# A graph network on one core: count and weight matrices by blocks of 8 destination nodes

## The reference

```python
# L0, three times: mean over the edges of each relation
seg = dst * R + etype
agg = segment_sum(x[src], seg) / max(count, 1)
h = relu(einsum('nrd,rdk->nk', agg, W) + h @ root + bias)
# L1: attention over edges, weight exp(-leaky_relu(s1[src] + s2[dst]))
h_prime = segment_sum(edge_e[:, None] * h[dst], src)
# L2: weighted sum over edges
agg = segment_sum(edge_weight[:, None] * x[row], col);  y = agg @ W.T + b
# L3: mean of edge attributes per node, then an MLP on [x, mean]
agg = segment_sum(edge_attr, col) / max(cnt, 1)
```

## Time and profile before

| | |
|---|---|
| median of 3 runs | 5356.65 us (5346.82 to 5359.11) |
| span of the profiled execution | 5385.6 us |
| PE busy | 4150.9 us, 77% |
| DVE busy | 2954.1 us, 55% |
| GpSimd busy | 3014.2 us, 56% |
| ScalarE busy | 964.9 us, 18% |
| front | 0 to 649 us |
| pass 1 | 649 to 1745 us |
| pass 2 | 1775 to 2757 us |
| pass 3 | 2773 to 3740 us |
| attention | 3740 to 4055 us |
| pass 4 | 4083 to 5215 us |

### The profile page before, as it was taken

How to read it: one execution, slowest core, us unless ns; L and a number is a source line. 1 busy time by engine, 2 the same in 40 slices (tenths; PEclk the granted TensorE clock), 3 DMA queues, 4 the chain that set the end, 5 groups by cost and what they waited for, 6 DMA issues and landing times.

```text
span 5385.6 us, 98227 instructions
## 1 busy us (share of the span) xinstructions
PE 4150.9 (77%) x20763; PEld 2938.9 (55%) x20764; DVE 2954.1 (55%) x6694; ACT 964.9 (18%) x3611; POOL 3014.2 (56%) x3064
## 2 busy tenths in 40 slices
PE   4777677778888788888878788887766988898863
PEld 1223265666666555555545555555665766676652
DVE  5444333333322677777777777877893333333335
ACT  0111111111111111111211111112441111111112
POOL 0000066666665677777767777775005777777750
PEclk7678778777777999999999999999785555656666
DMA  2011233333344222222322222322442333333320
GB/s 73 27 44 49 74 97 115 120 115 120 117 123 124 74 71 71 85 92 94 105 89 71 71 82 88 95 94 85 148 157 83 104 103 102 101 103 103 101 71 12
DMA packets 318265, 492.02 MB, mean 91 GB/s; under 512 B 98090, under 2 KB 221228, under 8 KB 314556
## 3 DMA queue, kind: packets, MB, share of 16 engines
q0 software_dynamic: 108864, 246.74, 16.0%
q1 hardware_dynamic: 209372, 244.94, 13.7%
HBM read 406.11 MB, written 85.29 MB: 91 GB/s over the span
## 4 chain that ended last, share of the span: by engine, by line
PE 30%; DMA 26%; issue 19%; POOL 12%; DVE 8%; DVEq 2%; ACT 2%; POOLq 1%; ACTq 0%; SPq 0%
DMA msg_r<-y_tab,idx_r 21%; POOL msg_r L494 12%; PE psum L1452 6%; DMA msg_r<-z_tab,idx_r 4%; PE psum L1387 4%; PE psum L1597 3%; PE psum L1598 2%; PE psum L1267 1%; PE psum L1279 1%; DVE hot_r L983 1%; DVE h_t L1142 1%; PE psum L1549 1%; PE psum L1399 1%; PE psum L1414 1%; PE psum L1299 1%
## 5 line engine op out<-in xcount | busy, mean ns | idle before, releaser
L494 POOL DMA_INDIRECT msg_r<-y_tab,idx_r x2160 | 2163.1, 1001 | 1561.7 <-issue 1185.3
L1452 PE MATMUL psum<-shot_r,hotb_r 128*128 128x400 bf16 x5760 | 1221.9, 335 | 359.2 <-DMA msg_r<-y_tab,idx_r 318.9
L494 POOL DMA_INDIRECT msg_r<-z_tab,idx_r x882 | 844.4, 957 | 630.8 <-issue 584.8
L1452 PEld LDWEIGHTS psum<-shot_r,hotb_r 128*128 128x128 bf16 x5760 | 480.3, 98 | 760.4 <-DMA msg_r<-y_tab,idx_r 404.0
L1007 DVE TENSOR_SCALAR shot_r<-iota_h,edge_g 128x1600 bf16<-128x1600 f16 x1440 | 893.6, 675 | 0.0
L570 ACT COPY idx_r<-row_i 128x1 int32 x2142 | 410.0, 191 | 2456.9 <-DMA msg_r<-y_tab,idx_r 2337.2
L1597 PE MATMUL psum<-msg_r,shot_r 128*128 128x128 f32 x1764 | 636.3, 460 | 143.7 <-DMA msg_r<-z_tab,idx_r 107.3
L1387 PE MATMUL psum<-hot_r,msg_r 128*128 128x128 f32 x2880 | 575.0, 358 | 194.3 <-DMA msg_r<-y_tab,idx_r 101.1
L1387 PEld LDWEIGHTS psum<-hot_r,msg_r 128*128 128x128 f32 x2880 | 486.5, 253 | 300.6 <-DMA msg_r<-y_tab,idx_r 158.3
L1597 PEld LDWEIGHTS psum<-msg_r,shot_r 128*128 128x128 f32 x1764 | 414.3, 292 | 339.2 <-DMA msg_r<-z_tab,idx_r 284.9
L1598 PE MATMUL psum<-msg_r,hot_r 128*128 128x128 f32 x1764 | 521.9, 396 | 0.0
(11 more groups left out here) (276 smaller groups left out, 3795.1 us busy)
## 6 DMA issues: line engine op xcount, KB each, us to landing
msg_r<-in_attr SPq DMA_DIRECT2D x882, 64.0 KB
h_t<-count_tab SPq DMA_DIRECT2D x25, 1600.0 KB, 6.5
count_tab<-w_s SPq DMA_DIRECT2D x48, 800.0 KB, 3.7
msg_r<-y_tab,idx_r POOLq DMA_INDIRECT x2160, 2.7
xn<-heavy_tab SPq DMA_DIRECT2D x76, 320.0 KB
y_tab<-y_s SPq DMA_DIRECT2D x25, 640.0 KB, 2.9
xn<-y_tab SPq DMA_DIRECT2D x25, 640.0 KB, 4.1
y_tab<-y_s SPq DMA_DIRECT2D x50, 320.0 KB
```

What stands on the lines that cost most here:

```text
L494: pool.indirect_dma_start(out=msg_r[:, q, 0:width], out_offset=None, in_=table, in_offset=bass.IndirectOffsetOnAxis(ap=idx_r[:, q:q + 1], ...
L1452: ins = T.matmul(psum[:, 4 + b, 0:CB], hotb_r[:, q, :], shot_r[:, q, b * CB:(b + 1) * CB], start=first, stop=last)
```

## The change

Count and weight matrices are built in another way, by *windows*: a window is 8 destination nodes (D8 = 8), and there are 384 (NW) for tiles 1 to 24. The edges of a window lie in a few neighbouring chunks, which are taken two at a time (VR = 2): one such step is a *visit*. For a visit DVE makes, for two chunks, `low` (the source's place within its tile, 128 columns), `key` (destination within the window times source tile, KW = 200 columns) and `weighted` (key times edge weight, 200), all f32, in one buffer `see_r`. PE multiplies `low` by the 400 columns of the other two and adds over the visits. So the first 200 columns are counts, the other 200 sums of weights. ScalarE copies both out of PSUM; the weights go to a new table `w_tab`; the counts are transposed on PE (`window_turn`), copied again and go to `count_tab`.

```diff
+            def window_hots(x):
+
+                w = x[2]
+                v0, v1, c0 = window_visits(dve, x)
+                behind = dve.snap(c0 - v0 * 2)
+                with dve.Fori(v0, v1) as v:
...
+                    dve.wait_ge(s_seen, v)
+                    V.scalar_tensor_tensor(out=key, in0=pair(KEY, KW), scalar=win_base[:, bass.ds(w, 1)],
+                                           in1=iota[:, None, 0:KW].broadcast_to([P, VR, KW]), op0=ALU.subtract, op1=ALU.is_equal)\
+                        .then_inc(s_key_hot, 1)
+                    V.tensor_tensor(out=low, in0=iota[:, None, 0:P].broadcast_to([P, VR, P]), in1=pair(LOW, P), op=ALU.is_equal)
+                    alone(dve)
+                    dve.wait_ge(s_key_hot, v)
+                    V.tensor_tensor(out=weighted, in0=key, in1=pair(WGT, KW), op=ALU.mult).then_inc(s_see, 1)
...
+            def window_sums(x):
+
+                v0, v1, _ = window_visits(pe, x)
+                alone(pe)
+                pe.wait_ge(s_turned, x[0] + 1)
+                clear(win_ps)
+                with pe.Fori(v0, v1) as v:
+                    alone(pe)
+                    pe.wait_ge(s_see, v)
+                    for i in range(VR):
+                        last = T.matmul(win_ps, see_r[:, i, 0:P], see_r[:, i, P:P + 2 * KW], start=False, stop=False)
+                    last.then_inc(s_seen, 1)
+                close(win_ps, s_wsum)
```

```diff
@@ PE, group_sums
+                    if q == UH - 1:
+                        if k < 3:
+                            window_sums(x)
+                if k < 3:
+                    window_turn(x)
@@ ScalarE, one_group
+                for q in range(U):
+                    if k == 2 and q % UH == 0:
+                        plain_ones(b, q // UH)
+                    if chunk is not None:
+                        next_row(k, of, c0, before16, q)
+                    if q == UH:
+                        window_out_of_psum(x)
+                    if q == UH + 1:
+                        window_store(x)
+                turned_out(x)
@@ PE, removed from passes 2 and 3
-                for b in range(4):
-                    ins = T.matmul(psum[:, 4 + b, 0:CB], hotb_r[:, q, :], shot_r[:, q, b * CB:(b + 1) * CB],
-                                   start=first, stop=last)
@@ DVE, removed from passes 2 and 3
-                    for q in range(half.start, half.stop):
-                        V.tensor_scalar(out=shot_r[:, q, :], in0=iota_h[:, :], scalar1=edge_g[:, SRC, q:q + 1], scalar2=None,
-                                        op0=ALU.is_equal)
```

```diff
@@ PE, pass 3
             def chunk2(q, slot, first, last):
-                count_sources(2, q, first, last)
+                T.matmul(attr_acc(slot), one_r[:, q, :], msg_r[:, q, P:2 * P], start=False, stop=False)
                 return T.matmul(acc(slot), hot_r[:, q, :], msg_r[:, q, 0:P], start=False, stop=False)
```

Pass 4 gathers only for tile 0 (27 groups), from x itself. Its groups are dealt out over 24 shares. In each share one tile D of 1 to 24 is computed as a product of x with the tile's 16 windows, loaded in one piece of 1.6 MB (128 × 16 runs of 800 bytes) into one of two slots; the weight matrix of L2 comes behind it:

```diff
+            def wide(t, slot):
+
+                pe.wait_ge(s_win_in[slot], t * 16 + 16)
+                for i in range(TILES):
+                    last = T.matmul(psum[:, 2 + slot, 0:P].rearrange("p (w d) -> p w d", w=WPT), xn[:, i, :], w_in[slot][:, :, i * D8:(i + 1) * D8],
+                                    start=i == 0, stop=i == TILES - 1)
+                last.then_inc(s_dense, 1)
+
+            def new_x(n, D, slot):
+
+                to = psum[:, 4 + slot, 0:P]
...
+                T.matmul(to, stage[:, slot, 0, :], l2w_s[:, :], start=True, stop=False)
+                T.matmul(to, ones[0:1, :], row("l2_b")[0:1, :], start=False, stop=False)
+                T.matmul(to, ident[:, :], xn[:, bass.ds(D, 1), :].rearrange("p o f -> p (o f)"), start=False, stop=True).then_inc(s_l2, 1)
```

More of the change, by code:

```diff
@@ L508, in _ @@
             pool.wait_ge(s_z_out, 16)
[L509 removed]
+            gather(3, x_tab, P, groups, 0)
         @block.scalar
@@ L598, in gathering @@
+                with act.Fori(begin + 1, TILES - 1) as D:
+                    tile(D)
+                tile(TILES - 1, ahead=False)
                 if table is not None:
```

662 lines of the change are left out of this document (434 added, 228 removed).

## The result

The changed kernel takes 7416.29 us, median of 4 runs (7396.35 to 7436.28), against 5357.88: a ratio of 1.384 (95% interval 1.380 to 1.388). The direction was forecast, the size was not: 2058 us more, not 723, and above the end of the range (6550).

The account below looks back on a forecast made before the run. Each pass was taken as a ring: a group costs the larger of the gathers' 7.5 us and the DVE-PE chain. 5385.6 + 955 + 343 + 258 - 860 + 25 = 6107, less 29: about 6080 us; range 5450 to 6550.

Parts of the forecast that it names:

- pass 4: Only 27 groups of tile 0 instead of 147: near 300 us, a change of -860 (bounds -925, -710).
- the attention stage: Between passes 3 and 4, the same count_tab loads hidden under the tile before: change 0, at most some 3 us later start.
- in pass 1 the mechanism: Pass 1: VectorE and TensorE work in series, 11.85 us per one-visit group, 3.95 per further visit; +955 (bounds +650, +1350).
- Rival (a): Passes 1 to 3: windows hidden under the gathers' 7.5 us per group, so faster, 4670 us; chance 0.15.
- Rival (c): Pass 4: window loads from 800-byte runs bound it, 14 to 18 us per tile, +40 to +130, 6150 us; chance 0.07.
- the sum keeps the row's 2.6: VectorE's prologue ahead of a window, four table reads and addresses: 2.6 us from a three-load row (bounds 1.6, 3.5).
- TensorE's reads counted at nothing: TensorE's own table reads ahead of a window in passes 1 to 3: no time in the sum.
- at the 0.77 of pass 1 about 2.05 with its start: TensorE's part of a visit, four matmul instructions: 1.5 us at high clock, 2.9 at low, taken as 2.05.
- Rival (b): All passes: TensorE falls to its low clock, visits 2.9 instead of 2.05 us, total 6900 us; chance 0.08.
- the chain of pass 3: Pass 3: ScalarE's plain_ones and work ahead add 1.8 to 2.1 us, 9.8 per group; +258 (bounds +35, +410).
- pass 2's chain: Pass 2: chunks 3 to 5, VectorE's half, prologue, hots, visit, close: 7.85 us per group; +343 (bounds +140, +470).
- the front: Ahead of the first matrix stage: 28 operations, 13.5 us, and a prefix sum with copies, 11.7; +25 (bounds +15, +30).

Follow-up runs that it names:

- the shorter reads: Changed kernel, reads left in place: fourth number read once ahead of the passes, TensorE skips chunk number, VectorE reads it without bounds; 7053.85 us against 7587.51.

## Why the prediction was right or wrong

**Right: the direction, pass 4 and the attention stage, and in pass 1 the mechanism.** There windows stand in a serial chain VectorE, TensorE, VectorE behind one buffer: the chain shows it, moving VectorE's reads gave back nearly the whole prologue, and with the buffer handed over in two halves a further visit got shorter. Rival (a), which put the group under 7.5 us, needed the opposite; with the reads and the place of the window mended, pass 2 still took 12.6 us per group. Pass 4 took 311 us for a predicted 300. Rival (c) did not occur: a window load took 8.0 us from issue to landing, a tile 13 us, and TensorE waited for such a load once, for 11.5 us. The loop behind pass 3, forecast to run 0 times, did run once (385 copies out, 581 visits for 579), some 16 us.

**Wrong: the prologue, "the sum keeps the row's 2.6".** It measured 3.98 us in pass 1, outside the upper bound of 3.5. The row was the right one; its transfer wasn't. Its three loads have no asserts. All four of the changed kernel's loads are bounded (`value_load(min_val=, max_val=)`), and the bound scaled the load count and forgot the asserts. Two of them cost 0.55 us in the kernel before, so four make about 1.1 of the 1.4 us, an estimate; the fourth load makes the rest. The Trainium skill's rule, weighed in the prediction and set aside ("DMA: Bandwidth & Descriptors", section "Latency and other measured facts"), gives about 600 ns per load. The chain has 0.31 us for the load alone, half of that, and from one load to the next, with its arithmetic and assert, 0.74 (1909.02 to 1909.76). Nor did the row agree with such a floor, as the prediction says: its three loads took 0.31 us each and came 0.45 apart. By the sum of the prediction 1.4 us in 384 windows is 530 us. The runs don't give it that much: moving the whole of VectorE's prologue gave 516, 446 of it in pass 1; in passes 2 and 3 TensorE's own reads stand beside VectorE's.

**Wrong: TensorE's reads counted at nothing.** They were not in the sum, and no reason was given. TensorE stood 790 us ahead of the clears. In pass 1 that lies beside VectorE's longer prologue; in passes 2 and 3 it is on the chain, as the shorter reads show.

**Wrong: the step "at the 0.77 of pass 1 about 2.05 with its start".** A visit took 2.87 us in pass 1, 2.84 in pass 2 and 2.21 in pass 3. The first two are near the low level's 3.0; a mean clock of a whole stage does not tell at which level a part of it runs. In 581 visits that is some 380 us. Rival (b) named this, with 0.08 of the chance. Its price for a visit, 2.9 us, was right in passes 1 and 2, but its sign, a granted clock near 0.5 through all three passes, did not come (0.70, 0.68 and 0.79). The prediction had seen in the earlier trace rows that the clock stood at 1.00 only beside the bf16 matmuls, and kept 0.77 nevertheless. In the kernel with neither those nor windows, pass 2 ran at 0.56.

**Wrong: the chain of pass 3.** The prediction took pass 2's chain and added ScalarE's part. TensorE waited only 25 us for VectorE in pass 3, so VectorE's prologue and hots were not in its row. ScalarE's part was, as it was said, here between the hots and the plain hots of one group:

```profile
5809.86 0.55 ACTq L688 DMA_DIRECT2D count_tab<-shot_r  x1
5810.81 0.52 ACT L701 ACTIVATE shot_r<-hot_r 128x384 f32<-128x384 f32 x1 [1.21 <-issue]
```

VectorE's hots were ready at 5809.83; `plain_ones` (L701) starts 1.0 us later, behind the window's store.

**The sum with measured prices.** Pass 1: 11.85 + 1.4 (prologue) + 0.95 (visit) + 0.7 (12 matmuls at 0.213) = 14.9; 120 × 14.9 + 130 × 5.1 = 2451, with the tiles' 114 to 228: 2565 to 2679, measured 2630. Pass 2: 7.85 + 1.2 + 0.95 + 0.3 = 10.3; 120 × 10.3 + 24 × 7.15 + 54 × 5.1 + 50 = 1733, measured 1708. Pass 3: 9.8 + 1.35 + 0.95 = 12.1; 120 × 12.1 + 11 × 5.1 + 30 = 1538, measured 1550 without the extra window. Only the first of these is borne out by the experiments. In pass 2 the number fits, but VectorE's prologue, which the sum has at 3.8 us per group, gave back 80 us in all when it was moved. In pass 3 the fit is luck: the sum has a chain that TensorE did not wait for, and with the visit's measured 2.21 it falls to about 1450. Apart from that, two sums of the prediction don't come out as written: its terms for pass 3 make 1249, not 1225, and rival (b)'s make 6930, not 6900.

**Wrong: the front.** 85 us to the first gather, not 25. The added operations took 29.5 (VectorE's first count at 93.2 us, not 63.7), the asserts 32, the longer step of the visits 23.

**The range** ended at 6550 since I took the bounds of the terms as independent. They hung on two prices, read and visit, each of which occurs in every window of three passes; my own sum of high ends was 6910. The read then lay beyond its end, the visit in passes 1 and 2 at it, and TensorE's reads had no term at all.

## What to carry to other kernels

Price a loop's sequencer work like an operation: count the loads, the asserts and the arithmetic between the last operation and the next, on each engine that has them, and look whether a wait hides them; here they were 4 us, more than all three hots. Don't price a short piece of TensorE's work by the mean clock of its stage: it runs at one of two levels, here 3.0 or 1.6 us for the same visit, so bound the sum by the low one. When a number fits, ask by an experiment whether the term is on the chain in each stage. And before a price is multiplied by every window of three passes, widen the range by that one price, in full.

## What was not expected of the hardware

- A loaded and bounded number costs VectorE's sequencer 0.74 us from load to load, of which the load is 0.31.
- In pass 2 without windows, where TensorE has small f32 matmuls between gathers, the granted clock is 0.56; before, with the bf16 matmuls beside them, it was 1.00.
- The chips differ: the kernel before takes 5350 to 5357 us on some and 6151 to 6161 on others, 15% more, the changed kernel 7423 and 7588, 2% more. Pass 4 of the changed kernel is 297 us on the first kind, at a DMA share of 0.72, and 361 on the second, at 0.59. What differs is open.
- The same loop of two operations steps in 1.43 us in one program and 1.68 in another, with the same instructions in the same order. The time is added around the loop's branch. Open.
